# Attention's key sums in three chains, its products with V in bursts of two steps

## The chip, the cores and the metric

The kernel runs on one core of one Trainium2 chip. The metric is the device time of one launch in microseconds (us), the median over several executions. The kernel before takes 4579.53 us (median of 3: 4577.45, 4579.53 and 4581.79).

## The reference

All data are float32. For x of 4 batches x 2048 tokens x 512 features the reference computes one transformer layer:

```python
h = layernorm(x)
q, k, v = h @ Wq.T + bq + ocr_bias, h @ Wk.T + bk, h @ Wv.T + bv      # 16 heads of 32
scores = q @ k.T / sqrt(32) + 0.1 * (|i - j| <= 2)                    # the band
x = x + (softmax(scores) @ v) @ Wo.T + bo
y, w = mx_quantize(layernorm(x)), mx_quantize(weight)                 # blocks of 32, a 6-bit grid
x = x + y @ w.T + bias
```

## The kernel before

The program has three stages, one after the other with a barrier between them: `project` (q, k, v; 0 to about 600 us), `attend` (about 600 to 4126 us) and `finish` (output projection, second norm, quantisation and linear layer; 4126 us to the end). Precision near float32 is had by splitting operands in a high and a low part.

`attend` works on 64 **units**. A unit is one group of 4 heads (HG) and one chunk of 512 queries (CH) of one batch; four units (QC = 4, one batch and head group) share their keys. A unit has 16 **steps** (KT), one for each 128 keys; two steps are a **macro** (m). A step is, on each engine:

- TensorE, `score` (L618): for each of the 4 heads one matmul of K^T and Q into the ring `ps_s` of 3 PSUM banks. The stationary side has a row of ones, and the row `ROWS` of `q_st` holds minus the maximum of each query, so that the scores come out shifted. After each score one matmul of `maximum` (L598) for the unit after the next few steps, into the ring `ps_m` of 3 banks; 64 such maxima are a unit's scores the other way round, from which VectorE finds the maximum of each query.
- ScalarE (L690): exp of each score, into `p_sb`, a ring of 8 steps (SLOTS).
- VectorE (L702): the maximum over each `ps_m` bank. On the 4 to 6 steps of a unit that touch the diagonal it multiplies the band's columns in `p_sb` by exp(0.1) or 1 (`spread_band`, L729).
- TensorE, `weigh` (L632): the product of `p_sb` of two steps ago with V, into `ps_o`. It uses column groups of 32, the 4 heads side by side; a float32 matmul is recorded as two instructions, so a step has 8.
- GpSimd (L772): for each macro `pair = p[2m] + p[2m+1]`. After every second macro it issues a DMA that adds one pair to the other in SBUF (L776, a **merge**, 1 MB). TensorE then multiplies the merged 4 steps by ones (`add_keys`, L642, 8 instructions as in `weigh`) into the bank `ps_d`: four times a unit, behind `weigh` of steps 1, 5, 9 and 13.

Once a unit, TensorE transposes the finished maxima (`turn`, L605), VectorE copies them to `shift` (L712), and SP sends them by DMA to the row of `q_st` (`put_shift`, L511). This happens in step 13; the first score of the next unit waits for the landing. The engines each execute their instructions in the order of the program; a wait holds up all that is behind it on its engine.

After a unit ScalarE copies `ps_o` and `ps_d` to SBUF; the sums go to DRAM, come back spread over the partitions, are inverted by VectorE, go to DRAM and come back as `rec_b`; GpSimd scales the output (L758), ScalarE rounds it to the high part (L675), GpSimd takes the low part (L762), and both are stored. For the last unit all of this comes before the barrier.

`finish` takes 16 chunks of 512 tokens. For each it loads the high and low part of the attention's output, projects (`out_project`, L979), adds, normalises and quantises on ScalarE and VectorE, transposes (`turn`, L988), and multiplies (`linear`, L1006).

## Time and profile before

| | |
|---|---|
| median of 3 runs | 4579.53 us |
| profiled execution, its own time | 4576.01 us |
| its span, first to last instruction | 4574.1 us |
| granted TensorE clock, mean | 0.985 of full speed |
| TensorE matmul busy | 4436.7 us (97%) |
| VectorE busy | 3378.5 us (74%) |
| GpSimd busy | 2828.9 us (62%) |
| ScalarE busy | 2446.5 us (53%) |

"Busy" is time in which an engine has an instruction under way; its share of the span says how near it is to be the bound, but a busy matmul is not one at its peak: the time from one start to the next in the timeline tells more than the duration of a record. A row "PE" is a matmul, "PEld" the load of its stationary operand, "SPq" the issue of a DMA. In brackets stands how long the engine was idle before, and what ended it.

### The profile page before, as it was taken

What the parts mean: (1) busy time and instruction counts of PE and PEld (TensorE: products, weight loads), DVE (VectorE), ACT (ScalarE), POOL (GpSimd) and SP (SyncE); (2) the same over time, 40 slices, a digit from 0 to 9 for tenths busy, and PEclk for the clock granted to TensorE, in tenths of its full rate; (3) what the DMA queues carried; (4) which work ended last, traced back from release to release, by engine and by line L of the source; (5) the groups of instructions that cost most, each with busy time, mean ns of one, the idle gap of its engine ahead of it and who ended that gap; (6) DMA issues with size and microseconds to landing.
All of it is one profiled execution on the core that took longest, in us unless ns stands there. A gap on an engine that the chain in (4) does not pass through costs nothing. (4 is left out here: it accounts for less than half of the span.)

```text
span 4574.1 us, 62800 instructions
## 1 busy us (share of the span) xinstructions
PE 4436.7 (97%) x22928; PEld 2504.6 (55%) x22928; DVE 3378.5 (74%) x5663; ACT 2446.5 (53%) x4652; POOL 2828.9 (62%) x927
## 2 busy tenths in 40 slices
PE   7999989999999999999999999999999999977999
PEld 6888845454445444444445454444454444525777
DVE  5444467888888888788787888888888788735776
ACT  2222216666666666666666666666666666651121
POOL 2111017778878787787877778878787787870000
PEclk9999969999999999999999999999999999988999
DMA  7666545555565656565656555565656565445452
GB/s 253 206 212 205 197 120 118 129 124 131 125 140 117 140 113 145 110 144 121 142 118 132 128 124 131 125 140 117 140 113 144 112 144 117 104 89 199 147 178 108
DMA packets 287700, 640.71 MB, mean 140 GB/s; under 512 B 40641, under 2 KB 107201, under 8 KB 249538
## 3 DMA queue, kind: packets, MB, share of 16 engines
q0 software_dynamic: 36864, 268.45, 29.3%
q1 hardware_dynamic: 250562, 368.66, 27.0%
q8 instruction: 165, 2.70, 0.2%
q14 instruction: 109, 0.89, 0.1%
HBM read 211.82 MB, written 156.24 MB: 80 GB/s over the span
## 5 line engine op out<-in xcount | busy, mean ns | idle before, releaser
L702 DVE TENSOR_REDUCE part_max<-ps_m 128x1 f32<-128x512 f32 x4096 | 2548.9, 683 | 654.0 <-PE ps_m L598 650.5
L772 POOL TENSOR_TENSOR pair<-p_sb 128x2048 f32<-128x2048 f32 x512 | 2348.4, 4587 | 665.5 <-ACT p_sb L690 301.9
L690 ACT ACTIVATE p_sb<-ps_s 128x512 f32<-128x512 f32 x4096 | 2114.8, 602 | 1130.3 <-PE ps_s L618 1129.8
L618 PE MATMUL ps_s<-q_st,k_st 97*128 97x512 f32 x4096 | 1732.4, 425 | 17.1 <-ACT p_sb L690 17.1
L598 PE MATMUL ps_m<-k_st,q_st 96*128 96x512 f32 x4096 | 1646.0, 405 | 42.0 <-POOL k_st L765 20.1
L618 PEld LDWEIGHTS ps_s<-q_st,k_st 97*128 97x128 f32 x4096 | 774.0, 189 | 1031.4 <-ACT p_sb L690 619.3
L632 PE MATMUL ps_o<-p_sb,v_sb 128*32 128x512 f32 x8192 | 1092.4, 605 | 0.2 <-DVE p_sb L729 0.2
L598 PEld LDWEIGHTS ps_m<-k_st,q_st 96*128 96x128 f32 x4096 | 785.7, 192 | 230.6 <-DVE part_max L702 76.3
L632 PEld LDWEIGHTS ps_o<-p_sb,v_sb 128*32 128x32 f32 x8192 | 161.3, 108 | 345.2 <-ACT p_sb L690 289.3
L166 POOL TENSOR_TENSOR xb<-xin,bo_row 128x2048 f32<-128x2048 f32 x16 | 75.3, 4706 | 424.7 <-DMA xin<-in_x 414.0
L642 PE MATMUL ps_d<-pair,ones 128*32 128x512 f32 x2048 | 267.5, 594 | 9.9 <-DMA pair<-pair 9.9
L776 POOL DMA_DIRECT2D pair<-pair x256 | 224.1, 875 | 81.8 <-POOL pair L772 73.1
L729 DVE TENSOR_TENSOR p_sb<-p_sb,band_f 128x520 f32<-128x520 f32 (+2 forms) x352 | 237.5, 701 | 14.6 <-ACT p_sb L690 14.6
L303 DVE SCALAR_TENSOR_TENSOR s_lo<-ps_p,bias,s_hi 128x512 fp32r<-128x512 f32 x128 | 96.0, 750 | 172.2 <-ACT s_hi L348 172.2
L348 ACT ACTIVATE s_hi<-ps_p,bias 128x512 fp32r<-128x512 f32 x128 | 88.2, 689 | 244.7 <-PE ps_p L399 239.8
L399 PE MATMUL ps_p<-x_hi,w_hi 128*128 128x512 f32 x512 | 204.1, 399 | 8.4 <-DVE x_lo L288 8.3
L399 PE MATMUL ps_p<-x_hi,w_lo 128*128 128x512 f32 x512 | 201.4, 393 | 0.0
L399 PE MATMUL ps_p<-x_lo,w_hi 128*128 128x512 f32 x512 | 200.6, 392 | 0.0
L642 PEld LDWEIGHTS ps_d<-pair,ones 128*32 128x32 f32 x2048 | 66.5, 110 | 163.4 <-issue 152.6
L873 ACT ACTIVATE t_hi<-ps_t 128x512 fp32r<-128x512 f32 x64 | 33.4, 603 | 204.6 <-PE ps_t L988 204.6
L313 DVE TENSOR_TENSOR v_st<-ps_p,bv_row 128x512 f32<-128x512 f32 x64 | 44.2, 692 | 120.0 <-PE ps_p L399 120.0
L979 PE MATMUL ps_r<-wo_hi,o_hi 128*128 128x512 f32 x256 | 102.2, 399 | 27.8 <-DMA o_lo<-o_lo_d 27.8
(94 smaller groups left out, 2678.4 us busy)
## 6 DMA issues: line engine op xcount, KB each, us to landing
pair<-pair POOLq DMA_DIRECT2D x256, 1024.0 KB, 7.3
q_st<-q_hi_d SPq DMA_DIRECT2D x128, 256.0 KB, 4.2
k_st<-k_hi_d SPq DMA_DIRECT2D x128, 256.0 KB, 5.5
xin<-in_x SPq DMA_DIRECT2D x16, 1024.0 KB, 8.2
xb_d<-xb SPq DMA_DIRECT2D x16, 1024.0 KB, 5.2
q_hi_d<-s_hi SPq DMA_DIRECT2D x64, 256.0 KB, 2.0
q_lo_d<-s_lo SPq DMA_DIRECT2D x64, 256.0 KB, 2.3
k_hi_d<-s_hi SPq DMA_DIRECT2D x64, 256.0 KB, 2.3
```

What stands on the lines that cost most here:

```text
L303: nc.vector.scalar_tensor_tensor(out=s_lo[:, n % RING], in0=ps_p[:, n % RING], scalar=bias[:, n // NHG, n % NHG:n % NHG + 1], in1=f32(s_hi ...
L399: last = nc.tensor.matmul(ps_p[:, n % RING], lhs, rhs, start=(k == 0 and j == 0), stop=(k == KB - 1 and j == 2))
L598: nc.tensor.matmul(ps_m[:, seq % RING_M, :], q_st[0:ROWS, u, h, t * P:(t + 1) * P], k_st[0:ROWS, g % 2, n, h, :], start=True, stop=True).t ...
L618: nc.tensor.matmul(ps_s[:, (HG * s + h) % RING_S, :], k_st[0:ROWS + 1, unit // QC % 2, kt // TT, h, kt % TT * P:(kt % TT + 1) * P], q_st[0 ...
L632: last = nc.tensor.matmul(ps_o[h * HD:(h + 1) * HD, :], v_sb[:, kt, h * HD:(h + 1) * HD], p_sb[:, s % SLOTS, h, :], start=(kt == 0), stop= ...
L642: last = nc.tensor.matmul(ps_d[h * HD:(h + 1) * HD, :], ones[:], pair[:, 2 * quad % PAIR_RING, h, :], start=(n == 0), stop=(n == QUADS - 1))
L690: nc.scalar.activation(p_sb[:, s % SLOTS, h, :], ps_s[:, (HG * s + h) % RING_S, :], ACT.Exp, scale=SCALE).then_inc(p_ready, 1)
L702: nc.vector.tensor_reduce(part_max[:, unit % 2, col, n:n + 1], ps_m[:, seq % RING_M, :], AX.X, ALU.max).then_inc(max_taken, 1)
L729: nc.vector.tensor_tensor(view, view, factor, ALU.mult).then_inc(banded, 1)
L772: nc.gpsimd.tensor_tensor(pair[:, m % PAIR_RING], p_sb[:, s % SLOTS], p_sb[:, (s + 1) % SLOTS], ALU.add).then_inc(paired, 1)
L776: pool.dma_start(pair[:, (m - 1) % PAIR_RING], pair[:, m % PAIR_RING], accum_op=ALU.add).then_inc(merged[m // 2 % 2], 16)
L979: last = nc.tensor.matmul(ps_r[:, t, :], lhs, rhs, start=(k == 0 and j == 0), stop=(k == NHG - 1 and j == 2))
```

## The change

Five edits in `attend` and one in `finish`:

1. **Burst.** `weigh` is no longer called after each step. In the middle of each odd step, ahead of its third head, `burst` runs `weigh` of two steps, one behind the other.
2. **Three chains.** GpSimd still forms 8 pair sums a unit. Pair n >= 3 now takes up pair n - 3 by a merge as soon as it is there, so there are 5 merges a unit in place of 4. The last three pairs hold all keys; `add_keys` multiplies these three by ones, once a unit, in the burst of step 7 of the next unit. The result goes into a bank of the ring `ps_m` (`sum_place`), not into `ps_d`, so `ps_m` gets the fourth bank.
3. **Rings.** `ps_m` 3 to 4 banks, `pair` 4 to 6 buffers, `p_sb` 8 to 6 steps.
4. **Bands.** Both bands of a macro are now put in together, after the second maximum of the step that follows the macro; before, one came ahead of and one behind a macro's 8 maxima.
5. **Epilogue of a unit.** The unscaled output is stored once (`o_d`), the sums too; they are inverted once per four units (`keys_of`), and for the last four in `finish`.
6. **`finish`** loads the unscaled output and, for each of 4 head groups, the inverse sums. GpSimd multiplies and takes the low part (8 instructions of 128x512 a chunk), ScalarE the high part (4 a chunk, `o_highs`); for chunk 0 VectorE does GpSimd's part. `out_project` waits for `o_split`.

```diff
-    RING_S, RING_M = 3, 3
+    RING_S, RING_M = 3, 4
-    SLOTS = 8
+    SLOTS = 6
     PAIRS = KT // 2
-    PAIR_RING = 4
+    PAIR_RING = 6
+    CHAINS = 3
+    MERGES = [(PAIRS - 1 - c) // CHAINS for c in range(CHAINS)]
+    SUM_AT = 7
...
             (SP, by step kt)
-                        if kt == 7:
+                        if kt == 8:
                             store_sum(unit - 1)
+                        if kt == 4:
+                            store_o(unit - 1)
...
             (TensorE)
+            def free_bank(place):
+                old = place - RING_M
+                if old in sum_places:
+                    pe.wait_ge(sum_copied, sum_places[old] + 1)
+                else:
+                    at_least(pe, max_taken, old + 1 - sums_to[max(old, 0)])
+                return place % RING_M
...
+            def add_keys(unit):
+                bank = free_bank(sum_place(unit))
+                for n in range(PAIRS - CHAINS, PAIRS):
+                    pe.wait_ge(merged[n % CHAINS], 16 * MERGES[n % CHAINS] * (unit + 1))
+                    for h in range(HG):
+                        last = nc.tensor.matmul(ps_m[h * HD:(h + 1) * HD, bank, :], ones[:],
+                                                pair[:, (PAIRS * unit + n) % PAIR_RING, h, :],
+                                                start=(n == PAIRS - CHAINS), stop=(n == PAIRS - 1))
                 last.then_inc(sum_done, 1)
+
+            def burst(s):
+                if 3 <= s < ST + 3:
+                    weigh(s - 3)
+                    weigh(s - 2)
+                if s >= KT and s % KT == SUM_AT:
+                    add_keys(s // KT - 1)
...
-            for s in range(ST + SUM_LAG - 3):
-                if s < ST:
-                    for h in range(HG):
+            for s in range(ST + SUM_AT + 1):
+                for h in range(HG):
+                    if s % 2 == 1 and h == HG // 2:
+                        burst(s)
+                    if s < ST:
                         score(s, h)
                         ahead(*max_at(s, h))
-                if 2 <= s < ST + 2:
-                    weigh(s - 2)
-                if s >= SUM_LAG and s % 4 == SUM_LAG % 4:
-                    add_keys((s - SUM_LAG) // 4)
...
             (ScalarE)
-            o_high(NU - 1)
+                    if h == HG // 2 and unit > 0:
+                        if kt == 1:
+                            copy_o(unit - 1)
+                        if kt == SUM_AT:
+                            copy_sum(unit - 1)
...
             (VectorE)
             for m in range(NM):
-                if m > 0:
-                    spread_band(2 * m - 1)
                 for s in (2 * m, 2 * m + 1):
                     for h in range(HG):
                         ahead(*max_at(s, h))
-                spread_band(2 * m)
+                        if h == 1 and s % 2 == 0 and s > 0:
+                            spread_band(s - 2)
+                            spread_band(s - 1)
...
             (GpSimd)
-                at_least(pool, sum_done, (m - PAIR_RING) // 2 + 1)
+                n, old = m % PAIRS, m - PAIR_RING
+                if old >= 0 and old % PAIRS < PAIRS - CHAINS:
+                    pool.wait_ge(merged[old % PAIRS % CHAINS], 16 * merges_to(old + CHAINS))
+                elif old >= 0:
+                    pool.wait_ge(sum_done, old // PAIRS + 1)
                 nc.gpsimd.tensor_tensor(pair[:, m % PAIR_RING], p_sb[:, s % SLOTS], p_sb[:, (s + 1) % SLOTS],
                                         ALU.add).then_inc(paired, 1)
-                if m % 2 == 1:
+                if n >= CHAINS:
+                    at_least(pool, merged[n % CHAINS], 16 * (merges_to(m) - 1))
                     pool.wait_ge(paired, m + 1)
-                    pool.dma_start(pair[:, (m - 1) % PAIR_RING], pair[:, m % PAIR_RING],
-                                   accum_op=ALU.add).then_inc(merged[m // 2 % 2], 16)
-                if m % PAIRS == 5 and m > PAIRS:
-                    scale_o(m // PAIRS - 1)
-                if m % PAIRS == 6 and m > PAIRS:
-                    o_low(m // PAIRS - 1)
+                    pool.dma_start(pair[:, m % PAIR_RING], pair[:, (m - CHAINS) % PAIR_RING],
+                                   accum_op=ALU.add).then_inc(merged[n % CHAINS], 16)
...
             (finish, SP: order of the first loads)
+            load_o(0)
             sp.dma_start(f32(wo_hi[:]), wo_hi_d).then_inc(wo_in[0], 16)
-            load_o(0)
             sp.dma_start(f32(wo_lo[:]), wo_lo_d).then_inc(wo_in[1], 16)
...
             (finish, GpSimd, for each chunk c from 1)
+                for g in range(NHG):
+                    nc.gpsimd.tensor_tensor(o_raw[:, b, g, :], o_raw[:, b, g, :], o_rec[:, b, g, :],
+                                            ALU.mult).then_inc(o_scaled, 1)
+                for g in range(NHG):
+                    pool.wait_ge(o_high, NHG * c + g + 1)
+                    nc.gpsimd.tensor_tensor(o_lo[:, b, g, :], o_raw[:, b, g, :], f32(o_hi[:, b, g, :]),
+                                            ALU.subtract).then_inc(o_split, 1)
...
             (finish, ScalarE)
+            def o_highs(c):
+                at_least(act, out_projected, TT * (c - 1))
+                for g in range(NHG):
+                    act.wait_ge(o_scaled, NHG * c + g + 1)
+                    nc.scalar.activation(o_hi[:, c % 2, g, :], o_raw[:, c % 2, g, :], ACT.Copy).then_inc(o_high, 1)
```

## Rows read from the trace of the kernel before

**Rows 1.** Windows view of a 400 us stretch inside attention

```profile
2000.00:2400.00 400.00, 396.35 (x2151) 198.88 (x2150) 325.74 (x542) 259.21 (x501) 318.69 (x104) 1.00 0.59 129
```

**Rows 2.** Timeline of TensorE inside attention: start us, us, engine, line, operation, count

```profile
2001.49 0.40 PE L598 MATMUL ps_m<-k_st,q_st 96*128 96x512 f32 x1
2001.82 1.06 PE L632 MATMUL ps_o<-p_sb,v_sb 128*32 128x512 f32 x8
2002.82 0.50 PE L618 MATMUL ps_s<-q_st,k_st 97*128 97x512 f32 x1
2003.16 0.40 PE L598 MATMUL ps_m<-k_st,q_st 96*128 96x512 f32 x1
...
2005.89 0.50 PE L618 MATMUL ps_s<-q_st,k_st 97*128 97x512 f32 x1
...
2011.02 1.07 PE L632 MATMUL ps_o<-p_sb,v_sb 128*32 128x512 f32 x8
2011.90 1.04 PE L642 MATMUL ps_d<-pair,ones 128*32 128x512 f32 x8
```

**Rows 3.** One line's view, L605: duration min/median/max in ns, first and last start

```profile
L605 PE MATMUL ps_m<-ident,neg_max x64: 273/277/407, 661.1 to 4034.2; 128*16 128x128 f32 x64
```

**Rows 4.** Timeline of TensorE's weight loads, last unit

```profile
4092.96 0.16 PEld L632 LDWEIGHTS ps_o<-p_sb,v_sb 128*32 128x32 f32 x8 [0.24 <-ACT p_sb L690]
...
4093.85 0.13 PEld L632 LDWEIGHTS ps_o<-p_sb,v_sb 128*32 128x32 f32 x4 [0.29 <-issue]
```

**Rows 5.** Timeline of TensorE and ScalarE in the last unit

```profile
4077.39 0.96 PE L618 MATMUL ps_s<-q_st,k_st 97*128 97x512 f32 x3
4078.66 0.50 PE L618 MATMUL ps_s<-q_st,k_st 97*128 97x512 f32 x1 [0.30 <-ACT p_sb L690]
...
4078.01 2.06 ACT L690 ACTIVATE p_sb<-ps_s 128x512 f32<-128x512 f32 x4 [0.63 <-PE ps_s L618]
```

**Rows 6.** Timeline of VectorE: maxima, the turned row's copy, bands

```profile
1996.34 2.48 DVE L702 TENSOR_REDUCE part_max<-ps_m 128x1 f32<-128x512 f32 x4 [0.44 <-PE ps_m L598]
1998.74 0.27 DVE L712 CAST shift<-ps_m 16x128 fp32r<-16x128 f32 x1
...
2025.25 1.31 DVE L729 TENSOR_TENSOR p_sb<-p_sb,band_f 128x520 f32<-128x520 f32 x2
...
4082.79 5.26 DVE L729 TENSOR_TENSOR p_sb<-p_sb,band_f 128x520 f32<-128x520 f32 x2 [2.52 <-ACT p_sb L690]
```

**Rows 7.** Timeline of GpSimd, one addition and the merge's issue behind it

```profile
1992.21 4.58 POOL L772 TENSOR_TENSOR pair<-p_sb 128x2048 f32<-128x2048 f32 x1 [0.98 <-ACT p_sb L690]
1997.08 0.87 POOL L776 DMA_DIRECT2D pair<-pair  x1 [0.30 <-DMA o_hi<-rec_d]
```

**Rows 8.** Shift row's issue on SP; landing times of that shift and that merge

```profile
1999.03 0.54 SPq L511 DMA_DIRECT2D q_st<-shift  x1
...
DMA to landing us min/median/max: 5.4/5.4/5.4
...
DMA to landing us min/median/max: 7.2/7.2/7.2
```

**Rows 9.** The page's DMA queues: packets, MB, share of 16 engines' span

```profile
q0 software_dynamic: 36864, 268.45, 29.3%
```

**Rows 10.** Timeline of TensorE and of SP's queue between the last two stages

```profile
4106.96 1.93 PE L642 MATMUL ps_d<-pair,ones 128*32 128x512 f32 x8 [9.90 <-DMA pair<-pair]
...
4109.59 0.53 SPq L524 DMA_DIRECT2D sum_d<-o_hi  x1
...
4126.16 0.33 SPq L842 DMA_DIRECT2D wo_hi<-wo_hi_d  x1
...
4136.70 0.79 PE L979 MATMUL ps_r<-wo_hi,o_hi 128*128 128x512 f32 x1 [27.81 <-DMA o_lo<-o_lo_d]
```

**Rows 11.** Timeline of one chunk of the last stage

```profile
4341.68 2.28 DVE L912 TENSOR_TENSOR xd<-y_q,qs 128x2048 f32<-128x2048 fp8e4 x1
...
4349.02 1.91 PE L988 MATMUL ps_t<-ident,xd 128*128 128x128 f32 x16
```

More of the change, by code:

```diff
@@ L456, in attend, with max_no, turn_no, sums_before @@
     bands_to = list(itertools.accumulate(int(near(s) is not None) for s in range(ST)))
-    def max_seq(unit, j):
+    def max_no(unit, j):
         return MAXES * unit + j + (unit - 1 + (j >= TURN_AFTER) if unit else 0)
-    def turn_seq(unit):
+    def turn_no(unit):
         return MAXES * (unit + 1) + unit + (TURN_AFTER if unit < NU - 1 else 0)
+    def sums_before(unit, j):
+        return max(unit - 2 + (j >= SUM_AFTER), 0)
+    def max_place(unit, j):
+        return max_no(unit, j) + sums_before(unit, j)
+    def turn_place(unit):
+        return turn_no(unit) + (sums_before(unit + 1, TURN_AFTER) if unit < NU - 1 else NU - 2)
+    def sum_place(unit):
+        return max_place(unit + 2, SUM_AFTER) - 1 if unit < NU - 2 else MAXES * NU + NU + unit
+    sum_places = {sum_place(unit): unit for unit in range(NU)}
+    sums_to = list(itertools.accumulate(int(place in sum_places) for place in range(sum_place(NU - 1) + 1)))
     def max_at(s, m):
@@ L579, in _ @@
                         put_shift(unit + 1)
[L580 to L583 removed]
+            sp.wait_ge(o_out, 16 * NU)
             sp.wait_ge(sum_out, 16 * NU)
[L585 removed]
+            sp.wait_ge(rec_out, 16 * (NG - 1))
         @block.tensor
         def _(pe):
+            def free_bank(place):
[5 more added lines that the diff above has]
+                return place % RING_M
             def maximum(unit, j):
@@ L792, in finish @@
         [sem(f"xb_in{i}") for i in range(2)], sem("fb_in"))
+    rec_in = [sem(f"rec_in{i}") for i in range(2)]
+    o_scaled, o_high, o_split = sem("o_scaled"), sem("o_high"), sem("o_split")
+    den_in, den_turned, rec_last = sem("den_in"), sem("den_turned"), sem("rec_last")
     fb_split, fb_ready, consts2 = sem("fb_split"), sem("fb_ready"), sem("consts2")
@@ L852, in _ @@
             sp.dma_start(f32(fb[1:2, :]), f32(fb_low[:])).then_inc(fb_ready, 16)
-            for c in range(2, NCH + 2):
-                if c < NCH:
-                    load_o(c)
-                    load_xb(c)
-                store(c - 2)
+            sp.wait_ge(den_turned, 1)
+            sp.dma_start(keys_of(rec_d, NG - 1), rec[:]).then_inc(rec_last, 16)
+            load_o(2)
+            load_o(3)
+            for c in range(NCH):
+                if c + 2 < NCH:
+                    load_xb(c + 2)
+                if c + 4 < NCH:
+                    load_o(c + 4)
+                store(c)
             for i in range(2):
@@ L864, in _ @@
             nc.gpsimd.memset(f32(ones2[:]), 1.0).then_inc(consts2, 1)
+            for c in range(1, NCH):
+                b = c % 2
+                if c == 1:
+                    pool.wait_ge(o_split, NHG)
+                pool.wait_ge(o_in[b], 16 * (c // 2 + 1))
+                pool.wait_ge(rec_in[b], 16 * NHG * (c // 2 + 1))
+                for g in range(NHG):
[5 more added lines that the diff above has]
+                                            ALU.subtract).then_inc(o_split, 1)
         @block.scalar
@@ L882, in normalise @@
                                          scale=rstd[:, t:t + 1]).then_inc(y_ready, 1)
+            def o_highs(c):
+                at_least(act, out_projected, TT * (c - 1))
+                for g in range(NHG):
+                    act.wait_ge(o_scaled, NHG * c + g + 1)
+                    nc.scalar.activation(o_hi[:, c % 2, g, :], o_raw[:, c % 2, g, :], ACT.Copy).then_inc(o_high, 1)
+            o_highs(0)
             act.wait_ge(consts2, 2)
@@ L886, in _ @@
             nc.scalar.activation(fb[0:1, :], fb_raw[:], ACT.Copy).then_inc(fb_split, 1)
+            o_highs(1)
             normalise(0)
+            o_highs(2)
             for c in range(NCH):
@@ L891, in _ @@
                     normalise(c + 1)
+                if c + 3 < NCH:
+                    o_highs(c + 3)
         @block.vector
@@ L943, in last_sum @@
                 nc.vector.tensor_tensor(res[:, c % 2, t, :], ps_r[:, t, :], x1[:, c % 2, t, :], ALU.add).then_inc(res_ready, 1)
+            v.wait_ge(o_in[0], 16)
+            v.wait_ge(rec_in[0], 16 * NHG)
+            for g in range(NHG):
+                nc.vector.tensor_tensor(o_raw[:, 0, g, :], o_raw[:, 0, g, :], o_rec[:, 0, g, :],
+                                        ALU.mult).then_inc(o_scaled, 1)
+            for g in range(NHG):
+                v.wait_ge(o_high, g + 1)
+                nc.vector.tensor_tensor(o_lo[:, 0, g, :], o_raw[:, 0, g, :], f32(o_hi[:, 0, g, :]),
+                                        ALU.subtract).then_inc(o_split, 1)
+            v.wait_ge(den_in, 16)
+            nc.vector.reciprocal(rec[:], den[:]).then_inc(den_turned, 1)
             v.wait_ge(fb_split, 1)
@@ L972, in out_project @@
                     for k in range(NHG):
+                        if t == 0:
+                            pe.wait_ge(o_split, NHG * c + k + 1)
                         toks = slice(t * P, (t + 1) * P)
```

155 lines of the change are left out of this document (58 added, 97 removed).

## The prediction

> **What bounds the kernel now.** I read the busy shares first, then windows, then the timeline. In a stretch of 400 us inside attention TensorE is busy for 396.35 us, VectorE for 325.74, GpSimd for 318.69 and ScalarE for 259.21, at full clock [rows 1]. So attention, some 3450 of 4574 us, goes at TensorE's pace, and the question is what sets that pace. The timeline of one step shows it [rows 2]: a step is 3.07 us (score at 2002.82, next step's at 2005.89). Within a run of full-array matmuls one starts every 0.235 us: from the maximum at 2003.16 seven more starts lead to the last one of that step, as they do to the last one of the step before, at 2001.49. Around the products with V there is more. Last maximum to first V: 0.33 (2001.49 to 2001.82); first V to next score: 1.00 (to 2002.82); that score to its maximum: 0.34 (to 2003.16). V followed by a sum's matmuls: only 0.88 (2011.02 to 2011.90). Check: 0.34 + 6 x 0.235 + 0.33 + 1.00 = 3.08.
>
> A unit should thus take 16 x 3.07 + 4 x 0.88 = 52.6 us. The transposes, one per unit, start at 661.1 the first and 4034.2 the last of 64 [rows 3]: 3373.1 / 63 = 53.54. The remaining 0.9 is the transpose (0.28 by its record) and some 0.65 of small stalls.
>
> **The change, part by part.**
>
> *Burst.* Two products with V in a row save one change into and out of the column groups: 0.33 - 0.235 = 0.10 before V, 1.00 - 0.88 = 0.12 behind it, 0.34 - 0.235 = 0.10 at the first score. That V behind V costs 0.88 too is shown once, at the end: loads for the first at 4092.96, the second at 4093.85 [rows 4]. A macro takes 0.34 + 14 x 0.235 + 0.33 + 0.88 + 1.00 = 5.84, against 6.14: 0.30 less, 8 times a unit: **-2.4 us a unit**.
>
> *Three sums in place of four,* always in a burst: one times 0.88 less, **-0.9**. The fifth merge costs TensorE nothing. The new unit without stalls: 8 x 5.84 + 3 x 0.88 + 0.3 = 49.6 us, against 53.54.
>
> *ScalarE's ring* (3 banks) now has to hold 8 scores without a pause. The last unit, which has no maxima, shows the loop: score at 4077.39, exps from 4078.01 (0.62 later) one per 0.517 (2.06 us for four), fourth score at 4078.66, 1.27 behind the first, as soon as the first exp is out [rows 5]. So score j can load its weights from 1.27 + 0.517(j - 3). With maxima between, it wants to at 0.47j - 0.135: equal at j = 3, 0.19 late at j = 7, of which about 0.13 is covered by the load's lead over its matmul (the load starts 0.235 before its matmul, and after a stall the matmul's record is only 0.10 longer). About 0.05 a macro: **+0.4 a unit**; none if the lead covers more, 0.19 x 8 = 1.5 if it covers nothing.
>
> *VectorE:* 8 maxima of 0.62 (2.48 for four) in 5.84 leave 0.9 us a macro; two bands cost 1.31 [rows 6]. Two macros of a unit have two full bands, so VectorE falls 0.4 us behind and then 0.8; the fourth bank takes the first up. The band is also later than now: its start is 0.77 + 4 x 0.62 = 3.24 after the run's first score, the first V of the burst at 3.95, and it needs the first band (0.69): just met without lag, late with it. I take **+0.6 a unit** for all of VectorE's lateness (0.65 of small stalls before, which had one bank less but 1.2 us of slack each macro), between 0 and what the nearest bad row gives, below.
>
> *GpSimd:* an addition takes 4.58, 0.3 later follows the merge's issue of 0.87 [rows 7]: 5.75 in a macro of 5.84, for 5 of 8 macros. It just fits, since scaling and low part (two instructions a unit) are gone. Where a band delays the start to 4.7 us into the run, the lag stays until macros without a merge; ScalarE needs the slot only 13.3 us into it, so `SLOTS = 6` leaves 3.8 us and costs nothing. If that cover went, ScalarE and then TensorE would wait.
>
> The row that speaks for more is the pair of bands that took 5.26 in place of 1.31, in the last unit, where they started while GpSimd was adding [rows 6]. By the Trainium skill (SBUF — State Buffer, "SBUF: two separate sides") a VectorE instruction with two SBUF inputs and a GpSimd instruction exclude each other, and the second waits for the whole of the first; that trace agrees, 1.31 against 5.26. By that rule the change is safe only while the previous addition has ended by 3.24 us into the run.
>
> By my sum it has, without a band in the macro before (start 1.8, end 6.4, next run at 5.84), and with one it ends 0.2 to 0.4 late (start 4.7, end 9.3 = 3.4 into the next). That is in the 0.6.
>
> *The shift row.* Before, the copy of it ends at 1999.01 and the issue is at 1999.03; its landing takes 5.4, that is 2004.4, and the merge issued at 1997.08 lands after 7.2, at 2004.3 [rows 6 to 8]. The two end together: the shift row sits behind the merge in flight. The score that needs it comes at 2005.89 [rows 2], so 1.4 us are in hand. The path from transpose to that score loses much: now V, a sum and two steps lie between; then one run and one burst. With the transpose in the second pair of the run, the issue is at 2.3 us into it and the score at 5.84 + 0.3 + 1.0 = 7.1. The merge of macro 5 issues at 0.9 of the same run in a unit whose bands are long past, lands at 8.1, and the shift with it: 1.0 us late. In units whose bands lie just before step 12, GpSimd's lag of 2.7 moves the merge to 3.6, behind the shift, and the one ahead lands by 5.2: no wait. The bands' place goes through the unit's number modulo 4; I take one to two units in four, **+0.5 a unit**, between 0 and 1.3.
>
> *DMA load.* A merge's packets take 29.3% x 4574 / 256 = 5.2 us of all 16 engines [rows 9]; five in 29 us are 90% of them, beside loads of keys and queries: the DMA share of 0.59 [rows 1] is 31.6 us a unit, 20.9 of it merges, 10.7 the rest. New: 26 + about 10 in 51 us, 0.7. The sums have 20 us until step 7, the chains 17 us per link against a landing of 7 to 9. Only the shift row feels it.
>
> Unit: 49.6 + 0.4 + 0.6 + 0.5 = 51.1, **-2.45 us, times 63 = -154**.
>
> *Last unit.* Without maxima ScalarE and GpSimd set the pace: 8 macros of 5.75 to 5.84 in place of 5.4 (a step is 1.27 to its fourth score [rows 5], then about 0.43 to V and 1.00 to the next score): +2 to +3, no saving.
>
> *Between the stages.* Before: last sum's matmuls at 4106.96, store at 4109.59, then inversion, scaling and stores until the next stage's first DMA at 4126.16: 16.6 us [rows 10]. New: store, its landing (an estimate of 2 to 3 us: less than the 5.4 of rows 8, since no merge is in flight), barrier: **-14**. First matmul of `finish`: 10.5 us after that DMA before (4136.70). New: 2 MB of output and inverse sums are asked for first (lands at about 7.5, an estimate: 4 MB were asked for before the first and third matmul could run, 10 to 13 us), four multiplications on VectorE (0.65 each, as half of the two bands in rows 6, which are as wide), a high part, a low part: 11 to 12. The third matmul waits for `wo_lo` as before. +1, between 0 and +8, as ScalarE's `o_highs(1)` and `o_highs(2)` stand ahead of work that chunk 0 waits for.
>
> *Chunks of `finish`.* TensorE is the bound; xd is ready at 4343.96, its transposes start at 4349.02 [rows 11]: 5.1 us of cover for what GpSimd's four low parts and four products (an estimate of 1.15 to 1.3 each: a quarter of the addition's columns and time, rows 7) can do to VectorE's quantisation by blocking it. I take 0; with the cover gone, 1 to 2 us in 15 chunks, +15 to +30.
>
> Sum on the profiled execution: 4576.0 - 154 + 2.5 - 14 + 1 = 4411.5. The median of the runs is 3.5 above that execution: **4415 us**.
>
> **The rivals.**
>
> A. *Nearly no stalls.* ScalarE's lead covers all, and GpSimd's lag keeps merges off the shift row: stalls 0.5 in place of 1.5 a unit. 4415 - 63 = 4352. For it: a fourth bank, and 1.2 us of idle VectorE time in each step now.
>
> B. *The band locks with the addition.* If GpSimd's lag does not die out, each addition ends later than 3.24 into the next run and each full band waits as in the 5.26 row: up to (5.26 - 1.31) less the 1.3 that the late part overlaps, about 2.6 us for one or two macros a unit, 2 more a unit on average: 4415 + 126 = 4541. Against it: the sum of 5.75 in 5.84, with three free macros to recover in.
>
> C. *Slower: the shift row falls behind two merges.* In place of the one in flight it also waits for the next (5.84 later, landing 7.2 after): 0.9 + 5.84 + 7.2 = 13.9 into the run in place of 7.1, 6.8 us a unit in place of 0.5: 4415 + 63 x 6.3 = 4812. It decides from 2.7 + 0.5 us of mean wait at the unit's first score on: then the kernel is no faster. For it: DMA at 90% in the merging half. Against it: the shift of rows 8 landed with the merge ahead of it, not after anything later.
>
> The Trainium skill (DMA: Bandwidth & Descriptors, "Queues, rings and completion order") has each DMA engine go round between queues, a packet of some 9 to 17 descriptors at a time. By that, a small row waits for one merge at most, as rows 8 have it, and C can't be; so I give C little.
>
> D. *The burst does not save the 0.30:* the gaps belong to something else, say a wait for the exps. Then 2.4 a unit are lost: 4415 + 151 = 4566. Against it: the V at 4093.85 behind a V has no such gap.
>
> **How the numbers follow.** Forecast 0.52, A 0.20, B 0.14, D 0.06, C 0.04, something between the forecast and no gain 0.04. The forecast's own range is 4380 to 4450. The range for 8 in 10 takes in A's time and part of B: 4345 to 4500. A difference of 0.2% is 9 us, about what can be told from none. Slower by more: C and the worst of D, 0.05. Within: 0.03. Faster: 0.92.
>
> **What would show it.** In attention's timeline: runs of 16 matmuls at 0.235, V behind V after 0.88, 5.84 from run to run; transposes 51.1 apart on average; a wait of about 1 us for the shift row in one or two units of four and of 0.05 for an exp late in a run; bands of 1.31, not 5; GpSimd's additions 5.8 apart in the merging half; 16.6 us between last sum's store and next stage down to 2 to 3. Wrong would be the forecast if the runs are broken by waits for VectorE or the bands, if the first score of a unit waits over 3 us, or if TensorE in `finish` waits for `o_split`.

## The result, and the profile after

| | before | after |
|---|---|---|
| median of the runs (4 each) | 4578.49 us | 4337.94 us (4337.17 to 4340.61) |
| ratio | | 0.947, 95% interval 0.9454 to 0.9486 |
| profiled execution, its own time | 4576.01 us | 4340.61 us |
| its span | 4574.1 us | 4338.8 us |
| granted clock, mean | 0.985 | 0.983 |

The kernel is 241 us faster. The forecast was 165 us, 4415 us; the time lies 7 us below the lower end of the range for 8 in 10 (4345), and rival A (4352) is the nearest. Six stretches of the two profiled executions show where the 235.3 us of span went. Each but the first and the last is the difference of two starts in the timelines:

| stretch | before | after | change | forecast |
|---|---|---|---|---|
| start to first transpose | 661.1 | 658.5 | -2.6 | 0 |
| 63 units, first to last transpose | 3373.1 (53.54 each) | 3124.7 (49.60 each) | -248.4 | -154 |
| last transpose to last sum | 72.8 | 75.5 | +2.7 | +2.5 |
| last sum to next stage's first DMA | 19.2 | 4.8 | -14.4 | -14 |
| that DMA to first matmul of `finish` | 10.5 | 24.4 | +13.9 | +1 |
| first matmul of `finish` to the end | 437.4 | 450.9 | +13.5 | 0 |

The transposes again give a unit's length. This is the view of their line (L605 has become L630; minimum, median and maximum of one, then first and last start), as [rows 3] before:

```profile
L630 PE MATMUL ps_m<-ident,neg_max x64: 272/275/407, 658.5 to 3783.2; 128*16 128x128 f32 x64
```

The same windows view as [rows 1], with the last unit's middle and the first 15 us of `finish` below it. Columns: window, its length, busy us of PE, PEld, VectorE, ScalarE and GpSimd, granted clock, DMA share, GB/s.

```profile
2000.00:2400.00 400.00, 397.56 (x2268) 223.71 (x2259) 336.89 (x579) 269.47 (x531) 332.20 (x106) 1.00 0.70 150
3785.00:3845.00 60.00, 58.05 (x241) 18.16 (x245) 9.47 (x5) 35.73 (x72) 47.61 (x17) 0.83 0.57 116
3863.00:3878.00 15.00, 0.00 (x0) 0.00 (x0) 0.00 (x0) 0.00 (x0) 0.23 (x2) 0.50 0.71 199
```

In the first window TensorE is idle for 2.4 us of 400 (3.65 before), and every other engine does more in the same time. The two lower ones come up below.

One macro on TensorE, as [rows 2]: start, duration, engine, line, operation, count.

```profile
1996.10 0.40 PE L624 MATMUL ps_m<-k_st,q_st 96*128 96x512 f32 x1
1996.34 0.28 PE L630 MATMUL ps_m<-ident,neg_max 128*16 128x128 f32 x1
1996.37 0.48 PE L643 MATMUL ps_s<-q_st,k_st 97*128 97x512 f32 x1
1996.69 0.39 PE L624 MATMUL ps_m<-k_st,q_st 96*128 96x512 f32 x1
...
2001.23 0.50 PE L643 MATMUL ps_s<-q_st,k_st 97*128 97x512 f32 x1
2001.57 0.40 PE L624 MATMUL ps_m<-k_st,q_st 96*128 96x512 f32 x1
...
2004.84 0.40 PE L624 MATMUL ps_m<-k_st,q_st 96*128 96x512 f32 x1
2005.17 1.92 PE L657 MATMUL ps_o<-p_sb,v_sb 128*32 128x512 f32 x16
2007.02 0.50 PE L643 MATMUL ps_s<-q_st,k_st 97*128 97x512 f32 x1
```

From 2001.23 to 2007.02 a macro is 5.79: 0.34 to the maximum, 3.27 for 14 starts, 0.33 to the burst and 1.85 for the 16 products to the next score. Forecast was 5.84, with 0.88 + 1.00 for the burst. The transpose delays its neighbours by 0.12 (0.59 from 1996.10 to 1996.69, where two starts take 0.47), not by 0.3. The burst with the three sums goes from 2022.56 to the next score at 2026.98, 4.42, which is 2.57 more than the 1.85 of a plain one. So a unit without stalls is 8 x 5.79 + 2.57 + 0.12 = 49.01, and 0.59 is left for stalls; forecast were 49.6 and 1.5.

The waits of TensorE in attention (us in total, times, the longest) name a part of these stalls. The first three rows are waits of matmuls, the last two waits of the loads before them:

```profile
PE ps_s L643 <- DMA q_st<-shift: 5.4, 10, 0.7
PE ps_o L657 <- DVE p_sb L752: 4.5, 18, 0.8
PE ps_o L657 <- ACT p_sb L715: 1.8, 11, 0.2
...
PEld ps_s L643 <- DMA q_st<-shift: 12.4, 15, 1.1
PEld ps_s L643 <- ACT p_sb L715: 1.4, 5, 0.4
```

Two mechanisms of the forecast are there, the shift row and the bands, and small: the matmuls' waits are 11.7 us in some 60 units, where 1.5 us in each were forecast. The third, the ring of scores, is all but absent: no score's matmul waited for an exp, and the loads before them 1.4 us in all. (The 1.8 us are products with V that waited for their exps.) The rest of the 0.59 doesn't show in these rows and stays open.

ScalarE and VectorE in these macros, as [rows 5] and [rows 6]; eight exps or maxima are one row:

```profile
2001.77 4.06 ACT L715 ACTIVATE p_sb<-ps_s 128x512 f32<-128x512 f32 x8 [1.76 <-PE ps_s L643]
...
2007.80 4.88 DVE L725 TENSOR_REDUCE part_max<-ps_m 128x1 f32<-128x512 f32 x8 [0.92 <-PE ps_m L624]
```

ScalarE rests 1.76 us a macro and VectorE 0.92 in one without bands. GpSimd's additions and the issues of its merges, the issue of the shift row on SP's queue, and the landing times of shift and merges, as [rows 7] and [rows 8]:

```profile
1993.04 0.88 POOL L795 DMA_DIRECT2D pair<-pair  x1 [0.55 <-POOL pair L790]
1994.05 4.58 POOL L790 TENSOR_TENSOR pair<-p_sb 128x2048 f32<-128x2048 f32 x1
1999.17 0.87 POOL L795 DMA_DIRECT2D pair<-pair  x1 [0.55 <-DVE p_sb L752]
1999.78 4.88 POOL L790 TENSOR_TENSOR pair<-p_sb 128x2048 f32<-128x2048 f32 x1
...
2005.82 4.90 POOL L790 TENSOR_TENSOR pair<-p_sb 128x2048 f32<-128x2048 f32 x1
...
1997.70 0.53 SPq L539 DMA_DIRECT2D q_st<-shift  x1
...
DMA to landing us min/median/max: 1.8/3.5/5.8
...
DMA to landing us min/median/max: 6.9/8.3/13.8
```

Where an addition starts right behind a merge's issue, the next comes 6.04 us later (1999.78, 2005.82), not 5.75: the addition takes 4.88 and the issue comes 0.55 behind it, not 0.30. That is more than a macro, so GpSimd falls behind there; it catches up in the macros without a merge. 228 of the 512 additions are of the long kind. The shift row was issued at 1997.70, 4.66 us behind one merge (1993.04) and 1.47 ahead of the next (1999.17).

### The profile page after: what moved, and what is told of

It is laid out like the page before. It is cut to its first block and busy times, and to the rows that moved or that the text cites. A ratio compares the mean times of both kernels' runs of the same rounds, so it can differ in the third digit from the quotient of the medians.

```text
span 4338.8 us, 61851 instructions
## 1 busy us (share of the span) xinstructions
PE 4207.4 (97%) x22416; PEld 2580.4 (59%) x22416; DVE 3304.7 (76%) x5623; ACT 2407.7 (55%) x4652; POOL 2934.3 (68%) x983
## 3 DMA queue, kind: packets, MB, share of 16 engines
q8 instruction: 161, 2.64, 0.2%
## 5 line engine op out<-in xcount | busy, mean ns | idle before, releaser
L725 DVE TENSOR_REDUCE part_max<-ps_m 128x1 f32<-128x512 f32 x4096 | 2513.4, 680 | 501.3 <-PE ps_m L624 501.1
L790 POOL TENSOR_TENSOR pair<-p_sb 128x2048 f32<-128x2048 f32 x512 | 2413.8, 4723 | 419.0 <-ACT p_sb L715 211.7
L643 PE MATMUL ps_s<-q_st,k_st 97*128 97x512 f32 x4096 | 1687.5, 413 | 8.8 <-DMA q_st<-shift 6.3
L657 PE MATMUL ps_o<-p_sb,v_sb 128*32 128x512 f32 x8192 | 994.4, 603 | 13.3 <-DVE p_sb L752 5.6
L624 PEld LDWEIGHTS ps_m<-k_st,q_st 96*128 96x128 f32 x4096 | 786.8, 192 | 189.0 <-DVE part_max L725 37.2
L657 PEld LDWEIGHTS ps_o<-p_sb,v_sb 128*32 128x32 f32 x8192 | 225.0, 109 | 495.0 <-ACT p_sb L715 315.1
L795 POOL DMA_DIRECT2D pair<-pair x320 | 280.2, 876 | 182.1 <-POOL pair L790 153.7
L752 DVE TENSOR_TENSOR p_sb<-p_sb,band_f 128x520 f32<-128x520 f32 (+2 forms) x352 | 192.5, 575 | 51.3 <-ACT p_sb L715 51.3
L905 POOL TENSOR_TENSOR o_lo<-o_raw,o_hi 128x512 fp32r<-128x512 f32 x60 | 125.8, 2127 | 134.7 <-ACT o_hi L930 134.7
L666 PE MATMUL ps_m<-pair,ones 128*32 128x512 f32 x1536 | 178.2, 595 | 9.1 <-DMA pair<-pair 9.1
L701 ACT ACTIVATE sum_st<-ps_m 128x512 f32<-128x512 f32 x64 | 38.2, 597 | 259.7 <-PE ps_m L666 259.7
```

What stands on the lines that cost most here:

```text
L624: nc.tensor.matmul(ps_m[:, bank, :], q_st[0:ROWS, u, h, t * P:(t + 1) * P], k_st[0:ROWS, g % 2, n, h, :], start=True, stop=True).then_inc( ...
L643: nc.tensor.matmul(ps_s[:, (HG * s + h) % RING_S, :], k_st[0:ROWS + 1, unit // QC % 2, kt // TT, h, kt % TT * P:(kt % TT + 1) * P], q_st[0 ...
L657: last = nc.tensor.matmul(ps_o[h * HD:(h + 1) * HD, :], v_sb[:, kt, h * HD:(h + 1) * HD], p_sb[:, s % SLOTS, h, :], start=(kt == 0), stop= ...
L666: last = nc.tensor.matmul(ps_m[h * HD:(h + 1) * HD, bank, :], ones[:], pair[:, (PAIRS * unit + n) % PAIR_RING, h, :], start=(n == PAIRS - ...
L725: nc.vector.tensor_reduce(part_max[:, unit % 2, col, n:n + 1], ps_m[:, max_place(unit, j) % RING_M, :], AX.X, ALU.max).then_inc(max_taken, 1)
L752: nc.vector.tensor_tensor(view, view, factor, ALU.mult).then_inc(banded, 1)
```

## The experiments

Each is an edit of the changed kernel, except the ninth; "unit" is the length by the transposes' line. The intervals are 95%.

| run | median us | ratio to before | unit us |
|---|---|---|---|
| changed kernel | 4337.94 | 0.947 (0.9454 to 0.9486) | 49.60 |
| e1_single | 4479.62 | 0.978 (0.9763 to 0.9796) | 51.92 |
| e2_three_banks | 4728.16 | 1.0318 (1.03 to 1.0335) | 55.84 |
| e3_old_bands | 4470.83 | 0.9759 (0.9743 to 0.9776) | 51.72 |
| e4_inverse_by_head | 4321.89 | 0.9433 (0.9418 to 0.9449) | 49.63 |
| e5_four_chains | 4500.86 | 0.9835 (0.9819 to 0.9852) | 52.12 |
| e6_two_chains | 4277.72 | 0.9349 (0.9333 to 0.9364) | 48.63 |
| e7_last_unit_single | 4338.36 | 0.9477 (0.9462 to 0.9493) | 49.67 |
| e8_early_shift | 4378.44 | 0.9567 (0.9551 to 0.9583) | 50.22 |
| e9_burst_alone | 4783.1 | 1.0448 (1.043 to 1.0465) | 56.56 |
| e10_two_chains_by_head | 4259.57 | 0.9302 (0.9287 to 0.9318) | 48.66 |
| e11_and_last_unit_single | 4257.23 | 0.9294 (0.9279 to 0.931) | 48.63 |

**The burst undone.**

```diff
                 if 3 <= s < ST + 3:
                     weigh(s - 3)
-                    weigh(s - 2)
...
-                    if s % 2 == 1 and h == HG // 2:
+                    if h == HG // 2:
                         burst(s)
```

> The changed kernel with the burst undone: in the middle of every step one product with V (of three steps ago), in place of two in the middle of each odd step; copy_o one step later. Theory: the gaps around a product with V are the price of going into and out of the column groups, 0.29 us per pair of steps (6.08 a macro in place of 5.79), 8 times a unit: +2.3 us x 64 = +150, about 4485. Rival (the burst saves nothing by itself, the gain came from the fourth bank and from stalls gone): 4340 to 4375.

Measured: +142 us, +2.32 a unit, which is 8 x 0.29. The gap around the products with V is what the burst saves, at the price that [rows 2] gave (0.30). The rival, that the gain is the fourth bank's and the stalls', would have left the time at 4340 to 4375.

**The fourth bank taken back.**

```diff
-    RING_S, RING_M = 3, 4
+    RING_S, RING_M = 3, 3
```

> The changed kernel with ps_m at 3 banks. Theory: a run is 8 maxima at 0.47 us apart and VectorE takes 0.60 for each; with three banks maximum j may load its weights when reduction j-3 is out, at 1.50 + 0.60(j-3), and would do so at 0.10 + 0.47j: 0.5 late at j = 7, of which 0.13 is covered. 0.38 a macro, 3 us a unit: +190, about 4530. Rival (the pause of the burst lets VectorE catch up, the fourth bank only takes up the bands): 0.5 us a unit, about 4370.

Measured: +390 us, +6.24 a unit, slower than the kernel before. The loads' waits in this run, then TensorE's timeline, then VectorE's:

```profile
PEld ps_m L624 <- DVE part_max L725: 711.5, 2005, 1.5
...
2003.45 0.50 PE L624 MATMUL ps_m<-k_st,q_st 96*128 96x512 f32 x1 [1.06 <-DVE part_max L725]
...
2026.15 3.39 PE L657 MATMUL ps_o<-p_sb,v_sb 128*32 128x512 f32 x16
...
2001.49 1.30 DVE L752 TENSOR_TENSOR p_sb<-p_sb,band_f 128x520 f32<-128x520 f32 x2
```

Two bands of 1.30 run while the scores' run goes on, and the maximum at 2003.45 finds no free bank. But the bands are only half of it. From one macro's first score to the next's the macros without a full band took 6.20 us in the median, 0.41 more than 5.79 and near the 0.38 of the theory; that is 2.5 us a unit for the six of them. The two with full bands took 1.64 more each at full clock, 3.3 us a unit, and this was not in the theory. The loads of the maxima waited 711.5 us for VectorE, in 2005 waits, against 37.2 in the changed kernel: with three banks VectorE's plain pace is too slow for a run of eight, and the fourth takes up both.

A part of the loss is the clock. Behind waits of 1.06 to 1.09 us in four macros one after the other the 16 products at 2026.15 took 3.39 in place of 1.92: the granted clock had fallen to the lower of its two levels, 1.2 in place of 2.4 GHz. Between the first and the last transpose it did so 29 times, 99 us in all; at 3.39 - 1.92 each this is some 43 of the 390 us, an estimate. The changed kernel has no such stretch there. The runs with four chains (14 times), the shift row earlier (7) and the burst alone (23) have them too, so their losses below are not of waits alone.

**The bands put back in their old places.**

```diff
+                if m > 0:
+                    spread_band(2 * m - 1)
                 for s in (2 * m, 2 * m + 1):
                     for h in range(HG):
                         ahead(*max_at(s, h))
-                        if h == 1 and s % 2 == 0 and s > 0:
-                            spread_band(s - 2)
-                            spread_band(s - 1)
+                spread_band(2 * m)
```

> The changed kernel with the bands at their old places in VectorE's program: in terms of a run of 8 maxima both now come behind the second of them, not behind the fourth. Theory: what counts is the place in the ring. Maximum 6 needs reduction 2, which comes 1.3 us later than without bands: 0.9 us of wait in each of a unit's two full macros, 1.9 a unit, +120, about 4460. Rival (the port: what counts is whether the bands run beside GpSimd's addition): records of bands of 3 to 5 us become common, and waits of TensorE for bands, +20 to +60. Third (the place is worth nothing): within 5 us of 4338.

Measured: +132 us, +2.12 a unit. The view of this run's bands, and its waits:

```profile
L752 DVE TENSOR_TENSOR p_sb<-p_sb,band_f x352: 144/693/4983, 673.1 to 3973.8; 128x520 f32<-128x520 f32 x64, 128x528 f32<-128x528 f32 x64, 128x8 f32<-128x8 f32 x48
...
PE ps_m L624 <- DVE part_max L725: 68.4, 111, 0.7
PE ps_s L643 <- DMA q_st<-shift: 15.6, 20, 2.2
```

The longest band before the last unit is 706 ns (the 4983 is in the last unit), so it is not GpSimd that holds them, and TensorE didn't wait for a band. It is the place in the ring, as the theory had it: where a macro has full bands, it is some 1.0 us longer (6.82 for 5.79), as the seventh maximum of the run waits for VectorE. A part of the 2.12 is the shift row, whose waits rose from 5.4 to 15.6 us.

**Inverse sums loaded by head instead of by head group.**

```diff
-                for g in range(NHG):
-                    sp.dma_start(o_rec[:, c % 2, g, :],
-                                 rec_d[g * NCH + c].unsqueeze(1).to_broadcast([HG, HD, CH]))
+                for h in range(HG):
+                    sp.dma_start(o_rec[h * HD:(h + 1) * HD, c % 2],
+                                 rec_by_chunk[c, h].unsqueeze(0).to_broadcast([HD, NHG, CH]))
```

> The changed kernel, whose last stage loads the inverse sums by head (32 partitions x 4 groups in one DMA) in place of by group (4 heads x 32 partitions); same bytes, same number of DMAs. Theory: the load by group, whose outermost dimension is 4, keeps only 4 of the 16 DMA engines busy (about 147 packets of 84 ns in 3 us are 4.1 engines), and this holds up the first matmul of the stage (24.4 us behind the stage's first DMA, 10.5 before the change) and chunk 1 (15.1 us of wait). By head it is spread over 16: first matmul after 12 to 13 us, the wait for chunk 1 under 5: -22 to -27, about 4314. Rival (the time is that of 2 MB more to land, or of VectorE's and ScalarE's added work): within 5 us of 4338.

Measured: -16 us, less than the 22 to 27 expected, the unit as in the changed kernel. SP's queue and the first matmul of `finish` in the changed kernel:

```profile
3863.54 0.37 SPq L850 DMA_DIRECT2D o_raw<-o_d  x1
3863.96 2.53 SPq L854 DMA_DIRECT2D o_rec<-rec_d  x4
3866.53 4.78 SPq L866 DMA_DIRECT2D wo_hi<-wo_hi_d  x1
...
3887.94 0.79 PE L1043 MATMUL ps_r<-wo_hi,o_hi 128*128 128x512 f32 x1 [27.27 <-DVE o_lo L1005]
...
3916.23 0.77 PE L1043 MATMUL ps_r<-wo_hi,o_hi 128*128 128x512 f32 x1 [15.06 <-POOL o_lo L905]
...
3892.00:3896.00 4.00, 4.00 (x19) 3.28 (x18) 2.62 (x5) 0.36 (x1) 0.00 (x0) 1.00 0.26 101
```

The last row is the windows view of 4 us within the second chunk's loads of the inverse sums: a DMA share of 0.26 is 4.2 of 16 engines. The queue and the matmul again, with the window of the stage's first 15 us, for the loads by head:

```profile
3865.73 0.38 SPq L851 DMA_DIRECT2D o_raw<-o_d  x1
...
3868.32 0.43 SPq L867 DMA_DIRECT2D wo_hi<-wo_hi_d  x1
...
3879.53 0.80 PE L1044 MATMUL ps_r<-wo_hi,o_hi 128*128 128x512 f32 x1 [16.68 <-DVE o_lo L1006]
...
3865.00:3880.00 15.00, 0.47 (x1) 0.47 (x2) 3.62 (x7) 2.44 (x4) 0.23 (x2) 0.50 0.87 273
PE ps_r L1044 <- POOL o_lo L906: 4.6, 2, 4.3
```

First DMA to first matmul falls from 24.4 to 13.8 us, and the second chunk's wait from 15.06 to 4.3; `wo_hi` is issued in 0.43 us where it took 4.78. The bytes are the same; the DMA engines are busy for 0.87 of the window in place of 0.71, at 273 GB/s for 199. The Trainium skill (DMA: Bandwidth & Descriptors, "Why a DMA increments its semaphore by 16 and not by 1") says that a transfer is spread over the largest number of DMA engines, up to 16, that divides the slowest dimension of both sides: 4 engines for the loads by group (4 heads), 16 for those by head (32 rows). The trace agrees: 4.2 engines are busy in the 4 us within the loads by group, the share and the GB/s rise by head, and the first matmul comes 10.6 us earlier. From the stage's first DMA to the end it is 19.4 us less in the profiled execution.

**Four chains.**

```diff
-    CHAINS = 3
+    CHAINS = 4
-    SUM_AT = 7
+    SUM_AT = 5
```

> The changed kernel with four chains in place of three (4 merges a unit, 4 products with ones, as many of both as before the change, but in one burst), summed at step 5. Theory: a product with ones in a burst is worth 0.88 us of TensorE, all of it on the path: +0.88 x 64 = +56, about 4394; one merge less a unit gives nothing back. Rival (the fifth merge costs something, by the shift row or the chains): +20 to +40. Rival (GpSimd now waits for the sums, as a pair's buffer is free only after them): over +80.

Measured: +163 us. GpSimd's waits, then TensorE's, in this run:

```profile
POOL pair L790 <- DMA pair<-pair: 285.0, 155, 5.7
...
PE ps_o L657 <- DVE p_sb L752: 56.6, 42, 3.8
```

In the changed kernel the first is 26.7 us in 34 waits. With six buffers and four of them held until TensorE has made the sums, GpSimd waits for a buffer, and V waits for the band. The bands themselves became longer: before the last unit 17 took over 2 us, up to 4.36, and in the changed kernel none. That is the record of rival B, a band of 5.26 in [rows 6], now in the steady state. That GpSimd's late addition holds the band is my reading of it; no run moves the one without the other. One more sum product is only some 0.9 of the 2.52 a unit.

**Two chains.**

```diff
-    CHAINS = 3
+    CHAINS = 2
```

> The changed kernel with two chains (6 merges a unit, 2 products with ones). Theory: TensorE has 0.88 us less a unit, a link of a chain has two macros, 11.6 us, for a landing of 8.3 in the median, and GpSimd 5.75 of work in a macro of 5.79: -56, less some 0.2 a unit of waits for the shift row, about 4295. Rival (the DMA engines: 6 merges of 5.2 us in six macros of 5.79, 90%, with loads beside them; links land late, GpSimd waits at its issues, ScalarE for its slots): no gain or slower, 4338 to 4450.

Measured: -60 us, -0.97 a unit: a product of 0.87, and waits for the shift row of 1.8 us in place of 5.4. A sixth merge a unit costs TensorE nothing, though the median addition is now 4876 ns (4614). The rival, six merges too many for the DMA engines, is out.

**The last unit without bursts.**

```diff
+                    if s > ST - KT + 1 and h == HG // 2:
+                        if s < ST + 2:
+                            weigh(s - 2)
...
-                    if s % 2 == 1 and h == HG // 2:
+                    elif s % 2 == 1 and h == HG // 2:
                         burst(s)
```

> The changed kernel whose last unit has one product with V in each step in place of bursts. In the changed kernel's last unit the granted clock falls to the lower of its two levels (0.83 of full on average over its 60 us, a burst takes 3.5 us in place of 1.85, a macro 7.1 in place of 5.5); the kernel before had 0.94 there. Theory: the burst leaves TensorE more idle time where no maxima fill the run, and the clock follows: singly it stays up and the unit takes as long as before the change, -6 to -10, about 4330. Rival (the clock falls anyway): within 3 us.

Measured: no change of the time, as the rival had it. But inside it: the last unit's 60 us have this row here,

```profile
3785.00:3845.00 60.00, 54.15 (x263) 18.21 (x263) 12.33 (x10) 41.34 (x82) 53.50 (x19) 0.94 0.64 132
```

against a granted clock of 0.83 with bursts, and the stretch from last transpose to last sum is 68.8 us, 6.7 less. The other 63 units took 0.07 more each in this run and the start 1.8 more, which gives the gain back; whether by chance of these runs is open.

**The shift row earlier.**

```diff
-    TURN_AFTER = 8
+    TURN_AFTER = 4
```

> The changed kernel with TURN_AFTER = 4: the maxima's row is transposed and sent one step earlier. My forecast had 0.5 us of wait a unit for this row; the trace shows 10 waits of 5.4 us in all. If the trace shows all of it: -3 to -6 at most. If the row cost 0.5 a unit in ways that the waits don't show (the DVE and ScalarE idle behind it): -20 to -30.

Measured: +40 us, and both theories missed: the shift waits are gone, yet a unit is 0.62 longer. TensorE's waits, TensorE, then VectorE in this run:

```profile
PE ps_m L624 <- DVE part_max L725: 16.4, 15, 1.2
...
2011.32 0.27 PE L630 MATMUL ps_m<-ident,neg_max 128*16 128x128 f32 x1
...
2013.65 0.49 PE L624 MATMUL ps_m<-k_st,q_st 96*128 96x512 f32 x1 [1.09 <-DVE part_max L725]
...
2011.69 1.31 DVE L752 TENSOR_TENSOR p_sb<-p_sb,band_f 128x528 f32<-128x528 f32 x2
...
2014.11 0.27 DVE L735 CAST shift<-ps_m 16x128 fp32r<-16x128 f32 x1
```

The transpose takes a bank of the same ring, and now late in a run: VectorE copies it out only at 2014.11, behind the two bands, and the run waits at 2013.65. The matmuls' waits for VectorE are only 16.4 of the 40 us; some 10 more, an estimate made as with three banks, are the clock: 7 stretches at the lower level. The rest lies with the loads, whose waits for VectorE before the maxima are 62.7 us (15.2 in the changed kernel), partly hidden.

**The burst alone, in the kernel before.**

```diff
+            def burst(s):
+                if 3 <= s < ST + 3:
+                    weigh(s - 3)
+                    weigh(s - 2)
+                if s >= SUM_LAG and s % 4 == SUM_LAG % 4:
+                    add_keys((s - SUM_LAG) // 4)
...
+                    if s % 2 == 1 and h == HG // 2:
+                        burst(s)
```

> The kernel before with the burst alone: both products with V of a macro, and the sum's product behind them, in the middle of odd steps; rings, sums, bands and epilogue as before. Theory: the burst saves 2.3 us a unit on the gaps, but makes runs of 8 maxima, which the 3 banks of ps_m don't carry: at 0.60 a reduction the last maximum of a run is 0.38 late, and the bands, which fall into the run, add about 1.5 in two macros: +5 to +6 a unit, net +3, slower than before, 4720 to 4800. Rival (the burst is worth its 2.3 us by itself): about 4435.

Measured: 204 us slower than before, 3.02 a unit. That is inside the expected range of 4720 to 4800. The burst's own gain (2.3) is there only with the fourth bank and the new place of the bands: taken singly from the changed kernel these cost 6.24 and 2.12 a unit.

**Two chains and loads by head.** The edits of the fourth and sixth together.

> The changed kernel with two chains and the inverse sums loaded by head, both together. The two act in different stages: if they add up, -60 - 16, 4262. Rival (they share something, say the phase of the last merges and the stage's first loads): 4270 to 4285.

Measured: 4259.57 us; the sum of the two single effects is 4337.94 - 16.1 - 60.2 = 4261.6.

**And the last unit without bursts.**

> As two_chains_by_head, with single products with V in the last unit. Single products held the clock and cut the last unit by 7 us in the trace, but the total did not fall. If those 7 us are real and were hidden by the spread between programs: 6 to 7 us below two_chains_by_head, run beside it here. If not: within 3 us.

Measured: 4257.23 us (4253.72 to 4258.63), against 4257.63 to 4260.42 without it. The spans overlap: no clear difference. Either is faster than both kernels.

## Why the prediction was wrong

**The failed step is the stalls of a unit:** "+0.4 a unit" for ScalarE's ring, "+0.6" for VectorE and the bands, "+0.5" for the shift row. They come to 0.59 in place of 1.5, which is 63 x 0.91 = 57 us. Another 37 us are the unit without stalls, 49.01 in place of 49.6: a macro is 0.05 shorter, the transpose costs 0.12 for 0.3, three sums 2.57 for 2.64. (The forecast's own terms add up to 49.66; 49.6 is rounded down.) Together they are the 94.4 us between forecast and measurement of this stretch. The sizes failed; two of the three mechanisms are in the trace, and the third is not.

*ScalarE's term* rests on a misread row. A row "x4" lasts from the first start to the last *end*: three spacings and one whole record. I divided it by four. An exp's record is 0.60, so the four of 2.06 in [rows 5] are 3 x 0.487 + 0.60, and an exp comes every 0.487, not 0.517; the eight of 4.06 after the change agree (3.46 / 7 = 0.494). With 1.27 + 0.487(j - 3), or 0.494, against 0.47j - 0.135 a run's eighth score is 0.06 to 0.09 late, inside the load's 0.13 of cover: no stall, and the scores' loads waited 1.4 us for exps in all.

*VectorE's term* was a guess, and the same misreading explains little of it. The four maxima of 2.48 in [rows 6] are 3 x 0.60 + 0.68, eight are 4.88, and 0.92 are left of a macro of 5.79, where I had 0.9. A band can start at 0.77 + 4 x 0.60 = 3.17 and is out at 3.86, against the burst 3.94 after the first score. The lag behind two bands was real by the sum (1.31 against 0.92), but the fourth bank took it up: V waited for bands 4.5 us in all, and no maximum's matmul waited for VectorE.

*The shift row* was right in mechanism and too large. It made loads wait for 12.4 us in 15 units of some 60, 0.2 a unit: one unit in four, at the low end of my one to two. The prediction put GpSimd at 5.75 in a macro of 5.84; it is up to 6.04 in 5.79. I had written this lag down as a danger; in the unit shown it puts the next merge behind the shift row, and the row now lands in 3.5 us in the median of all units (5.7 before). Rival A had named this; that the lag is the reason in all units was not tested. (Rival A also speaks of 1.2 us of idle VectorE time in each step; by [rows 6] it is 1.2 in a macro, 0.6 in a step.) That the longest landing is 5.8 also leaves nothing to C.

*The burst (-2.4) and the third sum (-0.9)* hold: e1 gives 2.32, e6 0.97 for one sum product with its shift waits. These are 3.2 of the 3.94 us a unit. The rest, some 0.7, is what the kernel before loses against e1 beyond the sum product (53.54 against 51.92, of which 0.87 is the sum). e1 has the new bank, bands, rings and epilogue; which of them takes the 0.7 away no run tells. D falls with e1.

*The edits don't add up.* Without the fourth bank the kernel is slower than before (e2), without the bands' place it loses 132 us (e3), and the burst alone costs 204 (e9). The prediction had the bank as a help against 0.6 us of lateness; it is worth 6.2 us a unit, the fallen clock included. That 8 maxima in a row are too much for three banks even without a band, the prediction doesn't say.

*Rival B* (bands locked with the addition) does not come about in the steady state: before the last unit 2 bands took over 1 us, the longest 1.53, where the kernel before had 45, up to 1.79. GpSimd's lag is there, but it recovers in each unit. In the last unit long bands can be seen, in VectorE's timeline:

```profile
3833.67 3.44 DVE L752 TENSOR_TENSOR p_sb<-p_sb,band_f 128x520 f32<-128x520 f32 x1 [1.79 <-ACT p_sb L715]
...
3840.73 3.99 DVE L752 TENSOR_TENSOR p_sb<-p_sb,band_f 128x528 f32<-128x528 f32 x1 [1.25 <-ACT p_sb L715]
```

*The last unit* has the forecast size, +2.7 for +2.5, by another cause. GpSimd's macro of 5.75 is not the bound; TensorE's clock fell to the lower of its two levels, 1.2 in place of 2.4 GHz, and the burst shows it, with score-ring waits between the runs:

```profile
3800.29 2.46 PE L643 MATMUL ps_s<-q_st,k_st 97*128 97x512 f32 x5 [0.22 <-ACT p_sb L715]
3802.68 3.57 PE L657 MATMUL ps_o<-p_sb,v_sb 128*32 128x512 f32 x16
...
3807.37 2.51 PE L643 MATMUL ps_s<-q_st,k_st 97*128 97x512 f32 x5 [0.22 <-ACT p_sb L715]
```

The 16 products took 3.57 in place of 1.92, and a macro 7.1 (3800.29 to 3807.37). e7, whose clock stayed at 0.94, took 68.8 us for 75.5, less than the 72.8 of before. The forecast's +2.5 was luck: a right number for a wrong reason.

*Between the stages* -14.4 for -14: right. *The start of `finish`* is a second term that was too small: +13.9 for +1, beyond the +8 I allowed; I had counted megabytes at the rate of the old loads, and not over how many DMA engines they go (e4: 10.6 of the 13.9). *The chunks* were not free: +13.5. The second chunk waited 15.06 for the same slow loads, and with the loads by head, where it waited 4.3, this stretch is 8.8 shorter. The 4.7 left are near the 4.6 us of waits that e4 still has there; no row here points to the port that I had weighed. These two stretches hid 26 of the 94 us, so the total missed by less than the unit did.

## What to carry to other kernels

Work out a spacing from merged rows as (duration - one record) / (count - 1): with eight in a row an error of 6% became a stall that wasn't there. A small stall can cost more than its own length, if the clock falls behind it. When instructions are gathered into longer runs, the buffer that feeds the consumer behind them and the place of that consumer's other work in the run decide: here the burst alone lost 204 us and with a bank and the bands moved it gained 142. When a load is reshaped, look at the outermost dimension it is split by, not only at its bytes.

## What the hardware showed that I had not expected

- GpSimd's addition took 4.59 us in some stretches and 4.88 in others, of the same shape; with two chains the median was 4876 ns, with three 4614. The 215 that began less than 0.7 us behind a merge's issue (as 1999.17 to 1999.78) took 4.87 to 4.92, and the 52 that began 0.9 us or more but under 2 us behind it (as 1993.04 to 1994.05) 4.51 to 4.59, so part of the 0.3 may lie in the record's start; what it is was not tried.
- A merge's issue on GpSimd came 0.55 us behind the addition, where the row of before had 0.30 [rows 7]. Why was not tried.
- The clock fell in the last unit although TensorE had matmuls under way for 58.05 of 60 us; with single products it was busy for 54.15 and held the higher level for more of the window (0.94 against 0.83). A part of the 58.05 follows from the clock, as records are longer at the lower level (3.57 for 1.92).
- With three banks the clock fell 29 times in attention, for some 3.4 us each; at 2026.15 this came behind four macros that each held a wait of 1.1 us. In the changed kernel it never fell there.
- Behind four issues of 0.6 us each the next on SP's queue, `wo_hi`, took 4.78; with the same bytes by head it took 0.43. What holds the issue was not tried.
